# Where TensorE spreads a set's column maxima in the key pass: first thing in the quarter, or behind other work

## The reference, cut to what matters

```
# Performer, key side                                  (per head, n runs over the 3125 nodes)
k, v     = split(x @ w_qkv.T)
k_prime  = exp(k*s @ proj.T - |k|^2*s^2/2 - m) + eps    # m: one maximum over everything
context  = k_prime.T @ v ;  k_sum = sum_n k_prime

# graph attention, layer 1, per target node d and head
e        = leaky_relu(al_s[src] + al_d[dst], 0.2)
ex       = exp(e - max over the edges of d)
out[d]   = sum(ex * row[src]) / sum(ex)
```

## Time and profile before

| | before |
|---|---|
| median of the timed runs | 3689.06 us (3686.57 to 3692.56) |
| span of the profiled execution | 4113.6 us |
| TensorE busy with matmuls | 3353.0 us, 82% of the span |
| VectorE busy | 1962.2 us, 48% |
| ScalarE busy | 1086.6 us, 26% |
| GpSimd busy | 1484.7 us, 36% |
| mean granted TensorE clock | 0.895 |

### The profile page before, as it was taken

One profiled execution on the slowest core, in us unless ns is written; L12 is line 12 of the kernel. 1 busy time (PEld: TensorE's weight loads), 2 busy tenths in 40 slices (PEclk: granted clock), 3 DMA queues, 4 the chain that ended last, 5 costly groups with the idle time before them and its releaser, 6 DMA issues. The chain is left out here.

```text
span 4113.6 us, 64799 instructions
## 1 busy us (share of the span) xinstructions
PE 3353.0 (82%) x22058; PEld 2653.8 (65%) x22059; DVE 1962.2 (48%) x4589; ACT 1086.6 (26%) x2387; POOL 1484.7 (36%) x1496
## 2 busy tenths in 40 slices
PE   5974899999898959999799994788888888569940
PEld 5863666666666648888799993455555555359940
DVE  6742555555555634444422222444444544453347
ACT  1322333333333323333311111222222221313321
POOL 1223556666566600000000004555555643223346
PEclk8986999999999979999899996998899899569975
DMA  5865677777767544444465647777777775736767
GB/s 194 304 230 175 215 227 225 234 228 227 233 218 232 182 157 138 127 148 133 145 78 78 79 68 253 261 245 257 260 255 262 258 249 172 244 113 234 245 221 254
DMA packets 279380, 828.66 MB, mean 201 GB/s; under 512 B 82606, under 2 KB 95633, under 8 KB 271542
## 3 DMA queue, kind: packets, MB, share of 16 engines
q1 hardware_dynamic: 182454, 408.38, 32.9%
q0 software_dynamic: 96640, 416.68, 32.3%
HBM read 699.01 MB, written 187.08 MB: 215 GB/s over the span
## 5 line engine op out<-in xcount | busy, mean ns | idle before, releaser
L928 POOL DMA_INDIRECT k_rows<-tab,k_pick x576 | 582.9, 1012 | 432.1 <-PE k_num L1371 243.7
L2118 POOL DMA_INDIRECT m_rows<-tab,m_e x500 | 489.6, 979 | 437.0 <-PE m_out L2421 231.9
L1371 PE MATMUL k_num<-k_rows,k_wt 128*32 128x384 f32 (+1 forms) x3200 | 339.8, 498 | 73.8 <-issue 49.2
L1371 PEld LDWEIGHTS k_num<-k_rows,k_wt 128*32 128x32 f32 x3200 | 110.8, 110 | 238.6 <-issue 198.5
L142 PE MATMUL g_prod<-g_w_hi,g_h_h 128*128 128x384 f32 x768 | 258.7, 337 | 0.0
L144 PE MATMUL g_prod<-g_w_hi,g_h_l 128*128 128x384 f32 x768 | 256.8, 334 | 0.0
L143 PE MATMUL g_prod<-g_w_lo,g_h_h 128*128 128x384 f32 x768 | 256.6, 334 | 0.0
L2421 PE MATMUL m_out<-m_rows,m_wt 128*32 128x384 f32 x2000 | 234.5, 557 | 10.4 <-issue 7.8
L1547 DVE TENSOR_TENSOR f_a_l<-f_turn,f_a_h 128x384 fp32r<-128x384 f32 x200 | 110.5, 553 | 277.1 <-ACT f_a_h L1519 276.5
L142 PE MATMUL f_prod<-f_w_hi,f_a_h 128*128 128x512 f32 x576 | 234.2, 407 | 0.0
L2401 PE MATMUL m_pj<-m_w,m_at 128*128 128x384 f32 x600 | 222.5, 524 | 13.0 <-DVE m_x L2213 10.6
(11 more groups left out here) (362 smaller groups left out, 7612.5 us busy)
## 6 DMA issues: line engine op xcount, KB each, us to landing
agg<-k_outb SPq DMA_DIRECT2D x100, 384.0 KB
f_a_in<-agg SPq DMA_DIRECT2D x100, 384.0 KB, 6.3
h<-f_e SPq DMA_DIRECT2D x25, 1024.0 KB, 4.3
g_h<-h SPq DMA_DIRECT2D x25, 1024.0 KB, 12.6
ys<-e_y SPq DMA_DIRECT2D x56, 384.0 KB, 3.3
tab<-q_xn SPq DMA_DIRECT2D x25, 388.5 KB, 6.8
tab<-g_row SPq DMA_DIRECT2D x25, 385.5 KB, 4.8
m_own<-tab SPq DMA_DIRECT2D x25, 385.5 KB, 8.6
```

The costliest lines, as they stand in the source:

```text
L928: pool.indirect_dma_start(rows[:, place(u, n), :], None, dram["tab1"], at, bounds_check=bound, oob_is_err=False).then_inc(rows_in[i], 16)
L1371: mm = pe.matmul(num[i][o, 0:n], wt[u % 2][:, v, o], rows[:, place(u, 2 * (half + v) + g), a:a + n], start=(v == 0), stop=(v == 1), tile_p ...
L2118: pool.indirect_dma_start(rows[:, place(h, c) + k, :], None, tab, bass.IndirectOffsetOnAxis(ap=e[h % 4][:, 0, k * SLOTS + c:k * SLOTS + c ...
```

## The change

Only TensorE's list in the key pass is changed. A set's spread leaves the head of the quarter. In turns 2 to 24 it stands behind the quarter's first `contexts` in quarters 0 and 1, and inside the product, behind the first two of its six chunks, in quarters 2 and 3. In turn 1, which has no contexts, it stands inside the product in all four quarters. In turn 25, which has no product, it stands behind the first `contexts` in quarters 0 and 1 and at the head in quarters 2 and 3. No instruction is added or removed, and no other engine's list is touched. 

```
+def product3_around(pe, out, x_hi, x_lo, w_hi, w_lo, between):
+    n = len(x_hi)
+    for k in range(n):
+        if k == 2:
+            between()
+        pe.matmul(out, x_hi[k], w_hi[k], start=(k == 0), stop=False)
+        pe.matmul(out, x_hi[k], w_lo[k], start=False, stop=False)
+        mm = pe.matmul(out, x_lo[k], w_hi[k], start=False, stop=(k == n - 1))
+    return mm
...
-                def product(t, c):
+                def product(t, c, between):
...
                     if t == 0:
                         product3_parts(*operands, wlo_done, KC * c).then_inc(gemm_full, 1)
+                    elif between is not None:
+                        product3_around(*operands, between).then_inc(gemm_full, 1)
                     else:
                         product3(*operands).then_inc(gemm_full, 1)
...
                         u, w = set_of(t, quarter), next_set(t, quarter)
-                        if u is not None:
-                            edge_spread(u)
                         if t >= 2 and quarter < 2:
                             contexts(t - 2, 2 * quarter)
+                        late = u is not None and 1 <= t < NT and (quarter >= 2 or t == 1)
+                        if u is not None and not late:
+                            edge_spread(u)
                         if t < NT:
-                            product(t, quarter)
+                            product(t, quarter, (lambda: edge_spread(u)) if late else None)
```

## The result

The changed kernel takes 3718.82 us (median of 4 runs, 3714.79 to 3720.59) against 3688.51 us before (4 runs): a ratio of 1.0078, interval 1.0066 to 1.0089. It is 30 us slower. I had forecast no change, 3686 us, with a range up to 3703 us.

The account below looks back on a forecast made before the run. TensorE's list was taken to set the pace, with 17.4 us of waits for `dg` within reach. Terms for quarters, product restarts and clock summed to -3.3 us, about 3686 us; own range 3678 to 3694, 8-in-10 range 3668 to 3703.

Parts of the forecast that it names:

- Quarter 1: Quarter 1's waits for `dg` disappear behind six context products, with no new wait for `zmax`: -8.0 us.
- Quarter 3: Quarter 3: `dg` waits go (-7.5), new `zmax` waits (+1.5), half the gain given back (+3.75), later values (+3.3 us).
- Quarter 0: Head of quarter 0: the spread, no longer covered by the wait for values, costs 0.32 us in 13 quarters: +4.2 us.
- Restarting the product: Products cut in two by the spread restart more slowly, 50 x 0.08 us: +4.0 us.
- The clock: Product matmuls on TensorE: three slow-clock stretches after long `dg` waits avoided, -4.5 us.
- B: Rival, head of quarter 0: the values' chain decides every turn, +12.0 us, 3701 us; chance 0.13.
- A: Rival, quarters 1 and 3: waits stay gone, values do not decide quarter 0, -14.5 us, 3674 us; chance 0.31.
- D: Rival, quarter 3: the spread waits inside the product instead, so nothing is gained there; about 3691 us; chance 0.06.
- C: Rival, quarter 1: GpSimd's addition stretches L1192 (+4.8 us) or L1186, delaying `zmax`; 3695 us; chance 0.08.

Follow-up runs that it names:

- b0: The kernel before, unchanged, traced again on the chip with stalls: 4171.63 us in its one run.
- c0: The kernel before, unchanged, traced again on a chip without stalls: 3695.20 us in its one run.
- b3: Against the kernel before, spread moved behind the first contexts in quarter 1 alone, on the chip with stalls: 4156.52 us, ratio 0.9981.
- e2: Against the kernel before, spread moved behind the first contexts in quarter 1 alone, on a chip without stalls: 3691.44 us, ratio 1.0002.
- c2: Against the kernel before, spread moved inside the product in quarter 3 alone, on a chip without stalls: 3708.49 us, ratio 1.0043.
- c3: Against the kernel before, spread moved behind the first contexts in quarter 0 alone, on a chip without stalls: 3696.80 us, ratio 1.0012.

## Why the prediction was wrong

**The step that failed** is the one that I had called the weakest: the sum was made on the profiled execution and its microseconds carried over unscaled. I had seen that its span was 424.5 us above the timed median and made the sum on it all the same. What that difference means could be suspected from the same rows: the edge sums stalled 75 times (49.2 us) with no releaser shown. Two of the sum's terms rested on these executions. The gain, 15.5 us of waits for `dg` in quarters 1 and 3, is there only beside the stalls: 29 waits in the first trace, 35 in b0, none behind the start of the pass in c0. The cost was halved, because in the first trace the values decided quarter 0 in 13 of 24 turns, TensorE being late by itself in the others; without stalls they decide it in all. So a gain was booked that was not there, and half of a loss was left out.

**Quarter 1, -8.0 us.** In keeping with b3 under stalls (-8, between 0.4 and 15), 0 in the timed runs (e2). That no new wait for `zmax` comes there was right: it is ready at 6.76 us, stretched by GpSimd's addition, and the turn is due at 7.41.

**Quarter 3, -7.5 + 1.5 + 3.75 + 3.3 = +1 us.** The mechanism was right: spread, shift, logits, `k_top`, scaled values, contexts of quarter 0. I gave 0.55 us a turn for the delay that is left; c2 shows 0.57 in quarter 0. The error is in the factor. I let the values decide half of the turns; they decide all 23, and the waits to be gained are 0 instead of 7.5 us. 23 x (0.57 + 0.08) = 15 us, measured +16. The new wait for `zmax`, +1.5 us, stands in no row; quarter 3 as a whole grew by 0.05 us a turn, 1 us, in after and by 0.08 in c2.

**Quarter 0, +4.2 us.** Right in size (+4.5, c3), though made of other factors: 0.21 us in every turn (0.19 us of spread behind the contexts) instead of 0.32 us in 13.

**Restarting the product, +4.0 us.** Too large: 50 cuts at 0.02 us make 1 us. The slower restart is there (0.26 us), but a spread between two matmuls of a product takes 0.14 us to the next start, not the 0.24 us of the one at the head of a quarter 2 or 3 (1021.89 to the product's first matmul at 1022.13), and pays for it:

```profile
692.70 0.38 PE L1376 MATMUL k_zbank<-k_dg,k_ones 128*128 128x128 f32 x2
692.84 0.42 PE L169 MATMUL k_gemm<-k_w_hi,k_xt_h 128*128 128x384 f32 x1
693.10 0.34 PE L170 MATMUL k_gemm<-k_w_lo,k_xt_h 128*128 128x384 f32 x1
```

**The clock, -4.5 us.** Nothing to give back: in the 23 turns it is at 1.00 before and after. This gain too was read from the first trace, where it was 0.95.

**The rivals.** B named the mechanism, the place and the condition ("as soon as TensorE loses less than about 0.5 us to stalls"), and its own argument for itself was the 424.5 us. It got 0.13 and 3701 us. Its 20.0 us for the chain are close to what was measured (19.7 to 22.9 in the 23 turns), in part by luck: the later values cost 0.65 instead of 0.55 us a turn and the uncovered spread 0.21 instead of 0.32. The 12 us that I took off for what quarter 1 and the clock still give were again read from the first trace. Without them it stands at 3713 us, 6 us under the result. A and D fall with the missing waits. C falls with e2: the addition stretches `zmax` itself, not one of the two operations that C names, and the turn does not wait. C's +4.8 us also took 0.2 us for 7.22 - 7.09 = 0.13. The forecast's own range was added too narrowly; the bounds of the restarts and the clock give 3674 to 3699 us, and the result lies outside that as well.

## What to carry to other kernels

Compare the span of a profile with the timed runs before reading anything else; where they differ as here (4113.6 against 3689.06 us), take another trace, or ask which idle times would be gone in the timed runs and read the kernel as if they were. A wait that exists only beside stalls is no gain, and slack that exists only beside stalls is no cover.

Before an instruction is moved later on an engine that has no idle time, follow what it releases all the way back to that same engine: here the loop goes over some 20 instructions of VectorE and ScalarE and takes 7.6 us (692.70 to 700.29), and it was 0.24 us too long before the change. Where such a loop closes, shorten the loop on the other engine: moving one pair of VectorE instructions into a gap that it had anyway gave 8.7 us, more than any place of the spread.

## What the runs showed of the hardware

One chip ran the same program in 4167.55 us (29 runs) and three others in 3691.74 to 3693.68 us, a difference of 13%. Two stretches of 100 us of the kernel before, 600 to 700 us, first on a chip with stalls (b0_before), then on one without (c0_before):

```profile
600.00:700.00 100.00, 88.66 (x669) 64.01 (x669) 55.90 (x166) 32.04 (x76) 57.70 (x57) 0.93 0.72 226
```

```profile
600.00:700.00 100.00, 99.38 (x849) 74.86 (x848) 67.24 (x212) 40.98 (x98) 74.64 (x71) 1.00 0.83 270
```

Every engine gets less done in the first: 669 matmul records instead of 849, at a clock of 0.93 instead of 1.00, with 226 instead of 270 GB/s. The 23 turns take 1017.4 us there and 823.1 here. What causes it, these runs do not tell, nor whether it stays with the chip: all runs on it were made together. The profiler alone does not do it, since the profiled execution there (4171.63 us) is as long as the timed ones and the one of c0 (3695.20 us) is as long as those of its own chip.

Two smaller things. A wait of 0.24 us between two groups of matmuls stands in no row, because the record of the spread (0.49 us) runs past the place where the next could have started (0.33 us); only the starts show it. And an fp32 matmul of 128 columns between two of a product costs 0.14 us to the next start, against 0.24 us behind the edge sums.
